# Preparation and table build joined in one block, norm sums moved into the build, filters shifted by one block

## The chip, the core and the metric

The kernel runs on one core of one Trainium2 chip. Its engines are TensorE (PE), VectorE (DVE), ScalarE (ACT), GpSimd (POOL) and the sync engine (SP), which issues most DMAs. The metric is the device time of one execution in microseconds; less is better.

## What is computed

A graph of 6,250 nodes with 128 features each and 200,000 edges sorted by their destination goes through two graph networks, each with a residual and a layer norm behind it. The first is three graph convolutions; the second makes a filter of every edge's weight, multiplies it with the source's features and takes the product over each node's edges.

```python
def graph_conv(x, W, b, act):                    # three times
    h = x @ W
    m = h[src] * norm_src[:, None]               # rsqrt of the out-degree, per edge
    agg = segment_sum(m, dst)
    out = agg * norm_dst[:, None] + b            # rsqrt of the in-degree
    return relu(out) if act else out
def product_net(h, edge_feat, dist):
    bf = exp(coeff * (dist[:, None] - centers[None, :]) ** 2)
    bf = ssp(bf @ W1 + b1)                       # ssp: softplus minus ln 2
    bf = ssp(bf @ W2 + b2)
    cut = where(dist < 5, 0.5 * (cos(pi * dist / 5) + 1), 0)
    agg = segment_prod(h[src] * edge_feat * bf * cut[:, None], dst)
    return ssp(agg @ W3 + b3)
x = layernorm(x + conv(conv(conv(x)))); x = layernorm(x + product_net(x, edge_attr, edge_weight))
```

## The kernel before

The program is a row of blocks. In a block each engine has an instruction list of its own, written out by hand or in loops, and the lists meet only in semaphores; at a block's end all engines meet. All DMAs of SP go through one queue in the order in which they stand; POOL's indirect DMAs (gathers) have another. There is no planner: the order in the text is the order of work on each engine.

**Preparation** (a block of its own, L142 to L260). SP loads the edges as 128 rows of 1,564: destinations (`e_dst`), sources, weights (`e_wt`), and the first destination of every chunk of 128 edges (`fd_i`, single words) and of every row (`e_next`). DVE packs destination and source into one word (`e_pk`, L212, L214), SP stores the packed edges to memory; DVE and ACT work out the cutoff factor of each edge (L216, the sine L248, L240 to L243) and whether an edge has the same destination as the one before it, PE turns the weights (L258), DVE copies them (L224) and SP stores them by step. Each such instruction is 1,564 elements wide.

**Table build** (the next block, L340 to L623). Chunk numbers come first: DVE splits `fd_i` (L403 to L408), makes one-hot rows of it (L411), PE counts them (L555), DVE copies the counts (L416) and sums them up to `chunk_i` (L424). With it POOL gathers 62 chunks of packed edges (L376), nine of them for the first of seven groups. `read_rows(j)` (L451 to L461) splits a group's words, ACT and PE turn them to tables (L514 to L523, L583). Then 28 loop turns of four steps follow: DVE makes the one-hots of a step (`hots`, L432 and L435), PE multiplies them (L599), ACT copies the counts (L540), SP stores them (L352), and PE adds them up for the out-degrees (L564). After the loop, behind each other: the source norms (L476 to L479, root L546), the segment sums of the counts (L483 to L488), the carries between rows (L491 to L493, PE L617 to L622), the pairs (L497, L498) and the step norms (L501, L502, root L548), which SP stores in three DMAs (L356 to L360). Then the block ends and the semaphores are cleared.

**Layers.** 48 blocks n, 16 for each of three layers. In each, PE multiplies the counts of 490 steps, in seven granules of 21 products (L957), with the nodes' features, kept in three bf16 parts `hps`. SP loads one granule ahead (L753). DVE scans the result (L1076), PE multiplies it with the layer's weights. Into the blocks n = 0 to 40 go the edge filters, two per block, at granules 0 and 1 (`slot`): ACT makes the basis of `dist` (L820, L822), PE two products (L932, L940), ACT and DVE the softplus. 82 filters are made there, the other 309 in the next stage. In block 0 the parts of `hps` don't exist yet: for each granule g, DVE scales x (L1092), ACT copies the first part (L868), DVE subtracts (L1100), ACT and DVE make the next two, and PE waits for them before granule g. POOL gathers 49 small tiles of `pairs` (L799) meanwhile; DVE turns them into `last_row` in block 1 (`last_rows`, L1105).

**Edges and end.** A straight stage over 391 blocks of 512 edges gathers node rows (L1306), makes the other filters (L1325 to L1449) and runs the products along (L1434, L1437). A last stage makes the second network's output.

## Time and profile before

| what | us |
|---|---|
| median of 3 runs (lowest, highest) | 5082.86 (5082.14, 5086.49) |
| profiled execution: its time, its span | 5105.77, 5104.0 |
| preparation, until its last DVE instruction ends | 33.5 |
| chunk numbers to the first one-hots of the loop | 33.8 to 76.86 |
| loop of the table build | 76.86 to 862.08 |
| sums behind it, block end | 862.08 to 874.84 |
| first block of the layers | 874.84 to 944.63 |
| other 47 blocks and what follows them | 944.63 to 2638.6 |
| edges | 2638.6 to 4985 |
| last stage | 4985 to 5104 |

In the whole span PE is busy 3802.7 us, DVE 3149.9, ACT 2755.1 and POOL 1897.5. In a table by stage each engine has its busy time and, in brackets, its instructions; PEclk is the granted clock of TensorE, 1.00 being full; then the busy share of the 16 DMA engines and the rate. In a timeline a row is one instruction or a run of like ones (x count): start, length, engine, line, output and inputs, shapes, and in square brackets how long the engine was idle before it and what ended that. SPq and ACTq rows are issues of DMAs, not transfers. A profiled execution takes a little longer than the ones that are timed.

### The profile page before, as it was taken

To read this page: it belongs to the slowest core of one execution; us is meant where nothing else is said; L and a number is where in the kernel's file an instruction comes from. 1 tells how busy PE (TensorE), PEld (TensorE's weight loads), DVE (VectorE), ACT (ScalarE), POOL (GpSimd) and SP (SyncE) were. 2 spreads that over 40 slices of the span, in tenths; PEclk is the share of its full clock that TensorE was granted. 3 is DMA by queue.
4 is the path that set the end of the run, shared out by engine and by line. 5 is a ranking of instruction groups with operands and counts; after the bars stand their busy time and mean duration, and the time that the engine had idled before them with its cause. 6 is when DMAs were issued, how large, how long until landed. Compare 5 with 4: busy or idle time off the path is not lost. (4 is left out here: it accounts for less than half of the span.)

```text
span 5104.0 us, 67054 instructions
## 1 busy us (share of the span) xinstructions
PE 3802.7 (75%) x22995; PEld 2424.4 (48%) x22995; DVE 3149.9 (62%) x5629; ACT 2755.1 (54%) x4313; POOL 1897.5 (37%) x1883
## 2 busy tenths in 40 slices
PE   3888887899999999999965665655656665566642
PEld 2777775444444444444434444443444444444432
DVE  7999997323232323232136777777777777777774
ACT  2666665222222222221017878877878787787863
POOL 4222001300100010001136666666666666666653
PEclk9888988999999999999976777777777677777775
DMA  3333333788877788877755555555555555555541
GB/s 108 132 136 129 126 130 133 227 240 248 243 232 240 244 246 242 255 242 235 224 145 157 171 166 172 167 171 170 168 164 173 172 172 165 166 169 167 172 141 54
DMA packets 641672, 920.47 MB, mean 180 GB/s; under 512 B 70098, under 2 KB 423239, under 8 KB 641431
## 3 DMA queue, kind: packets, MB, share of 16 engines
q1 hardware_dynamic: 550727, 782.65, 48.4%
q0 software_dynamic: 59936, 119.71, 8.8%
q10 hardware_dynamic: 30768, 15.26, 1.0%
q8 instruction: 107, 1.75, 0.1%
q14 instruction: 134, 1.10, 0.1%
HBM read 674.76 MB, written 242.59 MB: 180 GB/s over the span
## 5 line engine op out<-in xcount | busy, mean ns | idle before, releaser
L1306 POOL DMA_INDIRECT hgat<-x_rows,edge_src x1564 | 1497.4, 957 | 826.4 <-issue 453.4
L957 PE MATMUL bank<-gran,hp 128*128 128x490 bf16 x7056 | 1515.1, 373 | 26.6 <-DVE hp L1100 14.2
L957 PEld LDWEIGHTS bank<-gran,hp 128*128 128x128 bf16 x7056 | 678.0, 96 | 817.4 <-issue 29.6
L1373 PE MATMUL bank<-dist,v_sb 128*128 128x512 f32 x618 | 469.6, 849 | 737.9 <-issue 603.7
L1434 DVE TENSOR_SCALAR bank<-rows_e,edge_same,edge_first 128x128 f32<-128x128 f32 x1564 | 644.9, 412 | 121.7 <-DVE rows_e L1437 61.3
L810 POOL DMA_INDIRECT x_sb<-h_rows,last_i x147 | 139.2, 947 | 1540.6 <-DMA h_rows<-h_out 1473.8
L599 PEld LDWEIGHTS bank<-hi_hot,lo_hot 128*128 128x128 bf16 x7840 | 544.9, 155 | 223.3 <-issue 70.8
L599 PE MATMUL bank<-hi_hot,lo_hot 128*128 128x49 bf16 x7840 | 572.9, 219 | 101.4 <-DVE hi_hot L435 99.8
L540 ACT CAST stage<-bank 128x490 bf16<-128x490 f32 x784 | 451.9, 576 | 304.3 <-PE bank L599 304.3
L1386 PEld LDWEIGHTS bank<-v_sb,excess 128*128 128x128 f32 x2472 | 470.7, 262 | 281.8 <-issue 264.1
L1027 DVE TENSOR_SCALAR t<-bank,c_sb 128x512 f32<-128x512 f32 x82 | 61.5, 751 | 855.7 <-PE bank L932 848.3
L1386 PE MATMUL bank<-v_sb,excess 128*128 128x128 f32 x2472 | 477.9, 347 | 118.4 <-issue 117.6
L1437 DVE TENSOR_TENSOR rows_e<-bank,prod_e 128x128 f32<-128x128 f32 x1564 | 455.5, 291 | 163.2 <-DVE bank L1434 66.7
L432 DVE TENSOR_TENSOR lo_hot<-lo_t,rep_lo 128x8960 bf16<-128x8960 bf16 x112 | 539.5, 4817 | 9.9 <-issue 9.8
L1386 PE MATMUL bank<-v_sb,a 128*128 128x128 f32 x2472 | 434.3, 329 | 88.8 <-issue 88.8
L1373 PEld LDWEIGHTS bank<-dist,v_sb 128*128 128x128 f32 x618 | 117.7, 237 | 805.2 <-issue 662.4
L827 ACT ACTIVATE t<-t 128x512 f32<-128x512 f32 x82 | 51.0, 621 | 763.7 <-DVE t L1027 763.7
L1386 PEld LDWEIGHTS bank<-v_sb,a 128*128 128x128 f32 x2472 | 405.4, 246 | 113.7 <-issue 113.6
L1350 ACT ACTIVATE a<-bank,soft_max 128x512 f32<-128x512 f32 x309 | 208.5, 675 | 430.4 <-remote 409.0
L1445 DVE SCALAR_TENSOR_TENSOR bank<-bank,a 128x512 f32<-128x512 f32 x309 | 215.4, 697 | 218.9 <-ACT a L1355 115.1
L564 PE MATMUL bank<-stage,ident_b 128*128 128x490 bf16 x791 | 341.4, 433 | 0.4 <-ACT stage L540 0.4
L1419 DVE TENSOR_TENSOR prod_e<-hgat,efl 128x512 f32<-128x512 f32 x391 | 270.2, 691 | 37.7 <-DVE efl L1449 12.3
(239 smaller groups left out, 4313.9 us busy)
## 6 DMA issues: line engine op xcount, KB each, us to landing
gran<-step_counts SPq DMA_DIRECT2D x336, 857.5 KB
dist<-weight_by_step SPq DMA_DIRECT2D x391, 256.0 KB
running_products<-rows_e SPq DMA_DIRECT2D x391, 256.0 KB
step_counts<-stage SPq DMA_DIRECT2D x112, 857.5 KB
ef<-in_edge_attr SPq DMA_DIRECT2D x391, 224.0 KB
hgat<-x_rows,edge_src POOLq DMA_INDIRECT x1564
kn<-keep_and_norm_of_steps SPq DMA_DIRECT2D x48, 490.0 KB
edge_filter_times_attr<-g_out SPq DMA_DIRECT2D x82, 256.0 KB, 3.6
```

The costliest lines, as they stand in the source:

```text
L432: nc.vector.tensor_tensor(lo_hot[:, r], lo_of.unsqueeze(2).to_broadcast([P, 7, P, GS]), rep_lo[:].unsqueeze(1).to_broadcast([P, 7, P, GS]) ...
L540: nc.scalar.copy(stage[:, u % 2, :, g * GS:(g + 1) * GS], banks[f % 4][:, 0:GS * NT].rearrange("p (s h) -> p h s", h=NT)).then_inc(s_ev, 1)
L564: return nc.tensor.matmul(counts, ident_b[:], stage[:, r, :, g * GS:(g + 1) * GS], start=False, stop=False)
L599: last = nc.tensor.matmul(banks[f % 4][:, s * NT:(s + 1) * NT], lo_hot[:, u % 2, g, :, s], hi_hot[:, u % 2, g * GS + s, 0:NT], start=True, ...
L957: last = nc.tensor.matmul(y, hp[:, 7 * g + i, part, :], gran[:, g, :, i * IS:(i + 1) * IS], start=first, stop=last_)
L1306: pool.indirect_dma_start(out=hgat[:, b % U, c, :], out_offset=None, in_=x1_d, in_offset=bass.IndirectOffsetOnAxis(ap=edge_src[:, b, c:c + ...
L1373: nc.tensor.matmul(ps1[f % R][:], v1_sb[:], dist[:, f % Q], start=True, stop=True).then_inc(s_z14, 1)
L1386: last = nc.tensor.matmul(z[:, c * D:(c + 1) * D], part[:, f % R, c * P:(c + 1) * P], v2_sb[:], start=False, stop=part is a1 and c == C4 - 1)
L1419: nc.vector.tensor_tensor(prod_e[:, b % R], hgat[:, b % U], efl[:, b % U], ALU.mult).then_inc(s_v, 1)
L1434: nc.vector.tensor_scalar(factors[:, c], before, edge_same[:, b, c:c + 1], edge_first[:, b, c:c + 1], ALU.mult, ALU.add).then_inc(s_fac, 1)
L1437: nc.vector.tensor_tensor(rows_e[:, r, c, :], factors[:, c], prod_e[:, b % R, c, :], ALU.mult).then_inc(s_row if c < C4 - 1 else s_run, 1)
L1445: nc.vector.scalar_tensor_tensor(g, g, -LN2, a2[:, f % R], ALU.add, ALU.max).then_inc(s_g4, 1)
```

## The change

The preparation's block is gone. Its instructions stand in the table build's block, so there is one list per engine for both:

- SP loads `fd_i` first, then destinations, sources, `e_next`, weights; stores the packed edges, then loads x, then stores the turned weights.
- DVE does the chunk numbers' one-hots, then the packing, then copies the counts and makes `chunk_i`; then the preparation's other work, then the fills of `stage`, `rep_lo`, `rep_hi` and `strict`, then `read_rows(0)`, and behind it the four instructions of the cutoff factor. Ahead of the loop it waits for the stores of packed edges and weights.
- POOL gathers after `chunk_i` and after the store of the packed edges (a new semaphore, `s_pks`). PE turns the weights after its chunk counts.
- The preparation's tiles lie in space of `lo_hot`, `hi_hot` and `lo_t`.
- The segment sums (`count_sums`) stand in the loop, after group 5; the carries (`carries`) after the third of the four turns of group 6, whose loop is cut in two for it. PE's parts of both stand one piece ahead. After the loop there are the pairs, the step norms and then the source norms.
- In the layers, block 0 has no filters; the filters run in blocks 1 to 41 and their last steps in 42. SP issues the granules of block 0 first, then `kn`, c2, the filter weights and the first two `dist`. ACT makes the first basis ahead of its last copy in block 0. PE has block 1 written out in the first layer and its loop from block 2 on.

```diff
+            lent = lambda tile, start, n, dt: tile[:, start + 2 * EPP * n:start + 2 * EPP * (n + 1)].bitcast(dt)
...
+            e_in, number_k, e_ang = (lent(lo_all, FIRSTS, n, F32) for n in range(3))
+            iota_k = lent(lo_all, FIRSTS, 3, I32)
+            e_dst, e_pk = (lent(hi_all, 0, n, I32) for n in range(2))
...
+            e_wt = lent(lo_t, RB[1] * P, 0, F32)
...
+                    with nc.allow_non_contiguous_dma(reason="first dst of every chunk and of every partition"):
+                        sp.dma_start(fd_i[:, 0:whole], firsts[0:whole * P].rearrange("(t p) o -> p (t o)", p=P)
...
+                    load(e_dst, dst, s_dst)
+                    load(src_k, src, s_src)
...
+                    load(e_wt, edge_weight, s_wt)
+                    sp.wait_ge(s_pk, 1)
+                    sp.dma_start(pk_d.rearrange("(p k) -> p k", k=EPP), e_pk).then_inc(s_pks, 16)
+                    sp.wait_ge(s_iota, 1)
+                    sp.dma_start(run_d[ONES_ROW:ONES_ROW + 1, :], ones_row[:]).then_inc(s_prep, 16)
                     sp.wait_ge(s_xpad, 1)
                     sp.dma_start(x_sb[:, 0:NT - 1, :], x[0:(NT - 1) * P, :].rearrange("(t p) d -> p t d", p=P)
                                  ).then_inc(s_xin, 16)
                     sp.dma_start(x_sb[0:N - (NT - 1) * P, NT - 1, :], x[(NT - 1) * P:N, :]).then_inc(s_xin, 16)
+                    sp.wait_ge(s_wtc, -(-KT // 4))
+                    sp.dma_start(wt_d[0:(KT - 1) * P * P].rearrange("(j k p) -> k j p", k=P, p=P), wt_t[:, 0:KT - 1, :]
+                                 ).then_inc(s_prep, 16)
...
+                    nc.gpsimd.iota(iota_k, [[1, EPP]], base=0, channel_multiplier=0).then_inc(s_iota, 1)
                     pk_rows = pk_d.rearrange("(c e) -> c e", e=P)
                     pool.wait_ge(s_chunk, 1)
+                    pool.wait_ge(s_pks, 16)
...
+                    dve.wait_ge(s_fd, 48)
                     link(nc.vector.memset(fd_i[0:1, 0:1], PADNODE))
...
+                    dve.wait_ge(s_dst, 48)
+                    link(nc.vector.tensor_scalar(e_pk, e_dst, SRCBITS, None, ALU.logical_shift_left))
+                    dve.wait_ge(s_src, 48)
+                    nc.vector.tensor_tensor(e_pk, e_pk, src_k, ALU.bitwise_or).then_inc(s_pk, 1)
+
...
+                    dve.wait_ge(s_wt, 48)
+                    nc.vector.tensor_scalar(e_ang, e_wt, CUTOFF, None, ALU.min).then_inc(s_ang, 1)
+                    nc.vector.tensor_scalar(e_in, e_wt, CUTOFF, None, ALU.is_lt)
+                    nc.vector.tensor_copy(number_k, iota_k)
+                    link(nc.vector.tensor_tensor(e_same[:, 1:EPP], e_dst[:, 1:EPP], e_dst[:, 0:EPP - 1], ALU.is_equal))
...
+                    nc.vector.memset(stage[:, 1], 0.0).then_inc(s_zero, 1)
+                    nc.vector.tensor_copy(rep_lo[:], iota_f[:].unsqueeze(2).to_broadcast([P, P, GS]))
...
                     read_rows(0)
+                    dve.wait_ge(s_sin, 1)
+                    link(nc.vector.tensor_scalar(e_ang, e_ang, 0.5, 0.5, ALU.mult, ALU.add))
+                    link(nc.vector.tensor_tensor(e_ang, e_ang, e_in, ALU.mult))
+                    link(nc.vector.tensor_tensor(same_k, e_same[:], e_ang, ALU.mult))
+                    link(nc.vector.tensor_tensor(first_k, e_ang, same_k, ALU.subtract))
+                    dve.wait_ge(s_pks, 16)
+                    dve.wait_ge(s_prep, 16 * 3)
+                    def count_sums():
+                        dve.wait_ge(s_kt, 1)
+                        nc.vector.tensor_copy(kc[:], banks[4][0:ST, 0:2 * P].rearrange("r (a c) -> r a c", a=2)
+                                              ).then_inc(s_kc, 1)
+                        dve.wait_ge(s_kc, 1)
+                        nc.vector.tensor_tensor_scan(seg_sum[:], kc[:, 0, :], kc[:, 1, :], 0.0, ALU.mult, ALU.add)
+                        nc.vector.tensor_tensor_scan(kept[:], kc[:, 0, :], zeros_r[:], 1.0, ALU.mult, ALU.add)
+                        nc.vector.tensor_tensor_scan(row_sum[:], ones_f[0:ST, :], kc[:, 1, :], 0.0, ALU.mult, ALU.add
+                                                     ).then_inc(s_seg, 1)
+
+                    def carries():
+                        dve.wait_ge(s_tl, 1)
+                        nc.vector.tensor_copy(carry_c[:, 0:1], banks[6][0:ST, 0:1])
+                        link(nc.vector.tensor_copy(tails[:], banks[5][0:1, 0:2 * ST].rearrange("o (a r) -> o a r", a=2)))
+                        nc.vector.tensor_tensor_scan(carry_r[0:1, 1:ST + 1], tails[0:1, 1, :], tails[0:1, 0, :], 0.0,
+                                                     ALU.mult, ALU.add).then_inc(s_car, 1)
+
                     for j in range(7):
                         dve.wait_ge(s_te, fills_to[j])
-                        for a, b in ((4 * j, 4 * j + 1), (4 * j + 1, 4 * j + 4)):
+                        for a, b in parts_of(j):
                             with dve.Fori(a, b) as i:
                                 for u in range(4):
                                     dve.wait_ge(s_fill, i * 28 + 7 * (u + 1))
                                     hots(i, u)
                             if j < 6 and a == 4 * j:
...
+                            if j == 5 and a == 4 * j:
+                                nc.vector.memset(carry_r[0:1, 0:1], 0.0).then_inc(s_cnt, 1)
+                            if j == 5 and b == 4 * j + 4:
+                                count_sums()
+                            if j == 6 and b == 4 * j + 3:
+                                carries()
...
+                    act.wait_ge(s_ang, 1)
+                    nc.scalar.activation(e_ang, e_ang, ACT.Sin, bias=half_pi[:], scale=-math.pi / CUTOFF
+                                         ).then_inc(s_sin, 1)
...
+                    pe.wait_ge(s_const, 1)
+                    pe.wait_ge(s_wt, 48)
+                    for g in range(-(-KT // 4)):
+                        if g >= 3:
+                            pe.wait_ge(s_wtc, g - 2)
...
+                            if j == 5 and a == 4 * j:
+                                turn_counts()
+                            if j == 6 and a == 4 * j:
+                                ends_of_rows()
+                    pe.wait_ge(s_car, 1)
+                    nc.tensor.matmul(banks[6][0:ST, 8:9], carry_r[0:1, 0:ST], ones_f[0:1, 0:1], start=True, stop=True
+                                     ).then_inc(s_cc, 1)
...
-            FREE = FC // FB + 1
+            FREE = FC // FB + 2
...
-                return At(FB * n.const + g, n.reg, FB * n.step)
+                return At(FB * (n.const - 1) + g, n.reg, FB * n.step)
...
-                    load_dist(At(0))
+                    for g in range(NG7):
+                        load_granule(At(0), g)
+                    load_kn(At(0), At(0))
                     sp.dma_start(c2_all[:].rearrange("p (c d) -> p c d", d=D), c2.rearrange(
                         "(a b d) -> a b d", a=1, b=1).to_broadcast([P, C4, D])).then_inc(s_v, 16)
                     for tile, ap in ((c1_sb, col(c1)), (v1_sb, v1), (v2_sb, v2)):
                         sp.dma_start(tile[:], ap).then_inc(s_v, 16)
-                    load_granule(At(0), 0)
+                    load_dist(At(0))
                     load_dist(At(1))
-                    for g in range(1, NG7):
-                        load_granule(At(0), g)
-                    load_kn(At(0), At(0))
                     for tile, ap in zip(ws + bs, (w1, w2, w3, col(b1), col(b2), col(b3))):
                         sp.dma_start(tile[:], ap).then_inc(s_w, 16)
 
                     for n in range(3 * BLOCKS):
                         nxt = At((n + 1) % BLOCKS) if n + 1 < 3 * BLOCKS else None
                         for g in range(NG7):
-                            if g < FB:
+                            if n and g < FB:
                                 slot(filter_of(At(n), g))
                             if nxt is not None:
...
+                            if n == 0 and g == NG7 - 1:
+                                act.wait_ge(s_cst, 1)
+                                basis_of(At(0))
+                            if n and g < FB:
                                 slot(filter_of(At(n), g))
...
-                    pe.wait_ge(s_v, 16 * 4)
 
                     def one_block(k, n, first=False, filters=True):
                         for g in range(NG7):
-                            if g < FB and filters:
+                            if g < FB and filters and not (first and k == 0):
                                 slot(filter_of(n, g))
                             if first:
...
+                            pe.wait_ge(s_v, 16 * 4)
                             pe.wait_ge(s_w, 16 * 6)
-                        pairs_looped = max(0, min(BLOCKS - 2, FREE - 2 - BLOCKS * k) // 2)
+                            one_block(k, At(1))
+                        start = 1 if k else 2
+                        pairs_looped = max(0, min(BLOCKS - 1 - start, FREE - 2 - BLOCKS * k) // 2)
                         if pairs_looped:
                             with pe.Fori(0, pairs_looped) as it:
                                 for h in range(2):
-                                    one_block(k, At(BLOCKS * k + 1 + h, it, 2))
-                        after = min(BLOCKS, max(1 + 2 * pairs_looped, FREE + 1 - BLOCKS * k))
-                        for b in range(1 + 2 * pairs_looped, after):
+                                    one_block(k, At(BLOCKS * k + start + h, it, 2))
+                        after = min(BLOCKS, max(start + 2 * pairs_looped, FREE + 1 - BLOCKS * k))
...
+                    def first_bias():
+                        dve.wait_ge(s_v, 16 * 4)
+                        nc.vector.tensor_scalar(c1_less[:], c1_sb[:], -LN2, None, ALU.add)
+                        nc.vector.tensor_scalar(c1_over[:], c1_sb[:], -SOFT_MAX, None, ALU.add)
+                        link(nc.vector.tensor_scalar(c1_turned[:], c1_sb[:], -1.0, SOFT_MAX, ALU.mult, ALU.add))
...
+                                    first_bias()
```

## Rows read from the trace of the kernel before

**Rows 1.** Busy time by stage, table loop and first layer block; times in us.

```profile
core 0: us, PE busy (x) PEld busy (x) DVE busy (x) ACT busy (x) POOL busy (x), PEclk, DMA share, GB/s
...
76.86:862.08 785.22, 679.55 (x8730) 553.76 (x8730) 777.66 (x354) 478.02 (x824) 130.90 (x40) 0.88 0.32 128
...
874.84:944.63 69.79, 39.50 (x159) 17.27 (x160) 27.09 (x35) 22.41 (x29) 54.81 (x48) 0.72 0.74 210
```

**Rows 2.** Timeline of the preparation up to the loop: start, length, instruction, idle before.

```profile
start us, us, engine line op out<-in xcount [idle before <-releaser]
...
1.75 0.40 SPq L146 DMA_DIRECT2D e_dst<-in_dst  x1
...
4.11 0.40 SPq L160 DMA_DIRECT2D fd_i<-in_dst  x1
...
7.84 0.97 DVE L212 TENSOR_SCALAR e_pk<-e_dst 128x1564 int32<-128x1564 int32 x1 [4.50 <-DMA e_dst<-in_dst]
...
15.23 0.98 DVE L216 TENSOR_SCALAR e_ang<-e_wt 128x1564 f32<-128x1564 f32 x1 [1.83 <-DMA e_wt<-in_edge_weight]
...
31.70 1.79 DVE L243 TENSOR_TENSOR edge_first<-e_ang,edge_same 128x1564 f32<-128x1564 f32 x1
...
35.00 8.59 SPq L346 DMA_DIRECT2D x_sb<-in_x  x1
...
38.55 5.34 DVE L411 TENSOR_TENSOR lo_hot<-fd_f,iota_f 128x1664 bf16<-128x1664 f32 x4
...
45.37 0.21 DVE L416 COPY marks<-bank 128x49 f32<-128x49 f32 x1 [1.49 <-PE bank L555]
...
48.25 1.11 POOL L376 DMA_INDIRECT rows<-packed_edges,chunk_i  x1 [14.21 <-DVE chunk_i L424]
...
60.91 0.81 DVE L451 TENSOR_SCALAR ints<-rows 128x1152 int32<-128x1152 int32 x1 [12.70 <-DMA rows<-packed_edges,chunk_i]
...
65.74 1.36 DVE L461 SCALAR_TENSOR_TENSOR hi_b<-ints,mine 128x1152 bf16<-128x1152 int32 x1
...
66.16 1.75 POOL L376 DMA_INDIRECT rows<-packed_edges,chunk_i  x1 [0.30 <-issue]
...
76.86 4.83 DVE L432 TENSOR_TENSOR lo_hot<-lo_t,rep_lo 128x8960 bf16<-128x8960 bf16 x1 [9.76 <-issue]
```

**Rows 3.** Timeline behind the table loop: VectorE and SP.

```profile
866.11 0.42 DVE L483 COPY kc<-bank 62x256 f32<-62x256 f32 x1 [0.52 <-PE bank L615]
...
869.28 0.15 DVE L496 COPY carry_c<-bank 62x1 f32<-62x1 f32 x1 [0.36 <-PE bank L622]
...
871.61 0.22 SPq L360 DMA_DIRECT2D keep_and_norm_of_steps<-norm_s  x1
```

**Rows 4.** Timeline at the layers' first block; the last row groups line L799.

```profile
878.29 18.88 SPq L753 DMA_DIRECT2D gran<-step_counts  x6
...
886.74 0.15 DVE L1119 TENSOR_SCALAR c_less<-c_sb 128x1 f32<-128x1 f32 x1 [11.63 <-DMA v_sb<-in_L_gnn_W]
...
894.83 7.05 PE L957 MATMUL bank<-gran,hp 128*128 128x490 bf16 x21 [6.00 <-DVE hp L1100]
...
910.36 0.72 ACT L820 ACTIVATE dist<-dist,center 128x512 f32<-128x512 f32 x1 [15.88 <-issue]
...
916.01 28.78 PE L957 MATMUL bank<-gran,hp 128*128 128x490 bf16 x126 [12.38 <-issue]
...
918.96 1.09 DVE L1100 TENSOR_TENSOR hp<-x_sb,hp 128x896 bf16<-128x896 f32 x1 [1.00 <-ACT hp L868]
...
923.06 1.09 DVE L1100 TENSOR_TENSOR hp<-x_sb,hp 128x896 bf16<-128x896 f32 x1 [1.00 <-ACT hp L868]
...
946.38 4.57 PE L957 MATMUL bank<-gran,hp 128*128 128x490 bf16 x21
...
955.97 0.18 DVE L1105 TENSOR_SCALAR has_f<-pairs 128x49 f32<-128x49 f32 x1
...
L799 POOL DMA_INDIRECT pairs<-dges_up_to_and_in_degree,last_i x49: 943/947/1812, 875.5 to 945.3; - x49
```

**Rows 5.** Waits in the edge stage: who, for whom, us in total, times, longest.

```profile
engine line waited for: us in total, times, longest us
...
ACT a L1350 <- remote: 409.0, 79, 19.2
```

More of the change, by code:

```diff
@@ new lines, in _ @@
+                    nc.vector.scalar_tensor_tensor(e_row[:], pcol[:], float(EPP), at_row[:], ALU.mult, ALU.add)
+                    dve.wait_ge(s_next, 48)
+                    link(nc.vector.tensor_tensor(goes_on[:], e_next[:], e_dst[:, EPP - 1:EPP], ALU.is_equal))
+                    link(nc.vector.tensor_tensor(part_same[:], all_same[:], goes_on[:], ALU.mult))
+                    nc.vector.tensor_tensor(part_new[:], goes_on[:], part_same[:], ALU.subtract)
+                    nc.vector.tensor_scalar(part_one[:], goes_on[:], -1.0, 1.0, ALU.mult, ALU.add)
```

289 lines of the change are left out of this document (106 added, 183 removed).

## The prediction

> **What bounds the kernel now.** I read the table of stages first, then the timeline of each stage that the diff touches, then the waits of the rest. The profiled execution took 5105.77 us, a span of 5104.0 and 1.8 around it; the median of the runs shown is 5082.86. I work out the change on the profiled execution and take the sum off the median, 22.9 lower.
>
> The count-table loop is bound by VectorE: busy 777.7 of 785.2 us [rows 1]. Ahead of it stand 76.9 us in which no engine is busy for long: DMA, a chain of short VectorE work and nine gathers follow one another. The first block of the layers lasts 69.8 us with PE busy in 39.5 at a granted clock of 0.72 [rows 1]. The reader is to see three heads or tails in which everyone waits for a chain; the diff touches these three. In the rest PE (layers) and a chain over all engines (edges) set the time, with the same work before and after.
>
> **Part 1, the preparation.** Now it is a program of its own: packing from 7.84, e_ang from 15.23, last instruction 31.70 + 1.79 = 33.5; then chunk numbers, whose one-hots start at 38.55 and take 5.34; the first gather goes out at 48.25, the first rows are read at 60.91, the first large one-hot starts at 76.86 [rows 2]. The change puts the chunk numbers first.
>
> - Landing of fd_i: e_dst, issued first at 1.75, was used at 7.84, 6.1 later. fd_i now stands there, its issues taking 1.8 instead of 1.1. It is 1,563 single words, and its landing isn't visible before. Bounds: 6 (a little below e_dst) and 13.4 (all that packing waited for had landed). I take 8, the nearest row's value.
> - Splitting fd_i takes 0.9 (estimate: six small instructions of 0.15 to 0.2, linked), the one-hots 5.34: 14.3. Packing, 0.97 + 1.79, now stands behind them on VectorE: 17.1. PE's counting falls beside it. From one-hots to gather there are 4.4 us (43.89 to 48.25), of which the first 1.5 was the wait for that counting (45.37), so chunk_i is there at 17.1 + 2.9 = 20.0.
> - The gathers also wait for the store of the packed edges, issued at 17.1. It moves about as much as e_dst, whose load took 6.1 with the start of the queue in it; I take 3.9 (estimate), 6.1 at most: 21.0. So the first gather moves from 48.25 to 21.0.
> - VectorE's moved work between chunk_i and the first rows: from e_ang (15.23) up to the last four full-width instructions (one of 0.97, three of 1.79, so 33.5 - 6.4 = 27.1), 11.9, and the fills of stage and rep_lo, 2.5 (estimate): 14.4. It ends near 34.4, with PE's transposes beside it.
> - Nine gathers took 12.7 from first issue to first use (48.25 to 60.91). Now VectorE works beside them. At 66.16 a gather took 1.75 instead of 0.95 because it stood until the two-input instruction of 65.74 + 1.36 = 67.10 was over, plus 0.81 [rows 2]. The same was seen for gathers in the layers' first block: 49 in 70.8 us, up to 1.81 each [rows 4]. At that pace, one per 2 us while VectorE is busy, seven are out by 34.4 and the last two follow at 1.25: first use at 38.3. Bounds: 33.7 (no obstruction) and 47.1 (none gets through until VectorE is idle at 34.4).
>
> The Trainium skill, SBUF — State Buffer (Who interferes with whom) says that VectorE keeps GpSimd from writing descriptors only in a two-port mode, and that, as it infers, a tensor_tensor with both inputs in SBUF takes the read side alone and doesn't stop them. By it fewer of these instructions would obstruct and first use would be near 36. The row at 66.16 disagrees, as its blocker has two inputs, so I stay with 38.3.
>
> Reading the rows, then the tables through PE and ACT, then the first large one-hot: 60.91 to 76.86, 15.95, with 9.76 of VectorE idle in it [rows 2]. The last four full-width instructions of the preparation go into that idle stretch: 27.1 to 33.5, 6.4 us. They fit; were the idle gone, they would cost 6.4. The start of the loop moves from 76.86 to 54.3, a gain of **22.6** (13.8 to 27.2 by the bounds above).
>
> SP's queue: the load of x moves ahead of the stores of the weights and blocks SP for 8.6 (the 35.00 row). It starts at about 17.5, ends its issues near 27, and the weights' store follows, landing by 35. VectorE now waits for it before the loop, at about 51: 15 us to spare, cost nothing. The sine stands ahead of ACT's tables and is done by 24, long before them.
>
> **Part 2, the sums.** They used to stand behind the loop. From 866.11 to 869.28 VectorE makes the segment sums and carries, from 869.28 to 871.61 the pairs and norms until SP's last store is issued [rows 3]; the layers begin 3.2 later, at 874.84. The loop ends at 862.1 before and after. Moved into the loop, the first piece lengthens it, because VectorE is its bound: 3.2 at most, and 2.4 without the waits for PE (estimate; PE's answers are now long there). After the loop PE makes one small product, VectorE the same 2.3 us chain, then the store: 862.1 + 0.3 + 2.3 + 3.2 = 867.9, against 874.84. The source norms come next to it and end near 866, the last table store has landed by then. Gain 6.9 - 2.4 = **4.5** (bounds 2 and 7).
>
> **Part 3, the layers' first block.** Count from its start, t0 = 874.84.
>
> Now: VectorE waits until 886.74 for filter weights. PE starts at 894.83, runs one granule of 21 products in 7.05, then is idle 12.38 until 916.01, because ACT waited 15.88 for a dist that lay in the queue behind granules (910.36), and runs the other six in 28.78 [rows 4].
>
> Then: VectorE's first scaling starts at t0 + 0.5, and scale, copy, rest, copy, rest (1.09, 0.9, 1.09, 0.9, 1.09, one scaling between) give the first parts at t0 + 5.7. Granules go out each 3.1 (18.88 for six). The first, now issued first, lands by about t0 + 5.5 (3.1 and 2.4 to start, estimate); PE needs one each 4.57 (946.38). Parts come each 4.1 (918.96 to 923.06), also faster than PE. PE starts cold again (7.05 for the first) and takes 27.4 for six: block 0 ends at t0 + 40.2 instead of 69.8. The filter products that it held, one and a half slots of 1.75 (944.63, where block 1 begins, to 946.38), go to block 1: 2.6 [rows 1, 4]. All later filters shift by one block; one more block at the end carries them, one at the start doesn't, so their sum is unchanged. Gross gain 29.6 - 2.6 = 27.0.
>
> What is late next:
>
> - The first dist now stands behind seven granules, kn, c2 and the weights. In the old order c2 and the weights, all issued before the granules, were there only at 886.74, 11.9 after t0 with one dist ahead. I get t0 + 22 for the granules, 31 for dist. ACT wants it in front of its last copy; that makes the last part ready at t0 + 34.1, and PE wants it at t0 + 35.6. 1.5 to spare, up to 4 lost if dist comes 5 later.
> - POOL's 49 pair gathers took 70.8 (875.5 to 946.3) and were needed 11.3 after block 0's end (955.97). VectorE now wants them at t0 + 51.5 and, denser work beside them, gets them at t0 + 76 (15 in the first 31 us, the other 34 at 1.25, 2 to land). Behind last_rows on VectorE stand the filter steps and the scan of block 2. PE wants the first of these at t0 + 77.7. One block of slack swallows the wait but for 0 to 4.
>
> I take 1.7 for both: **25.3** (bounds 18 and 28).
>
> **Sum.** 22.6 + 4.5 + 25.3 = 52.4: 5053.4 in a profiled execution, 5082.9 - 52.4 = **5030.5** as the median.
>
> **Rivals.**
>
> 1. Gathers stand still behind VectorE until 34.4 (first use 47.1). For: the 66.16 row. Against: in the layers' first block they got through one by one between VectorE's instructions. Gain 43.6: 5039.3.
> 2. The head of the layers is held by dist or the pairs. For: both are later than needed by their old order. Against: a block of slack. Up to 7 more: about 5037.
> 3. The loop starts earlier: the 9.76 idle has no instruction of ACT's or PE's filling it fully, and fd_i may land at 6. Up to 6 more: 5025.
> 4. Slower than before: the edge stage. Its code is straight, and its ACT stood 79 times, 409 us, before one line's instruction, 5.2 each, on something the profile can't name [rows 5]. All code ahead of it changes length. From ten such stands more (10.1 x 5.2 = 52.4) the gain is gone; fifteen more give 5030.5 + 78 = 5108.5. Against: the runs of before lie within 4.4 us, so such misses are not loose, and the stage's instructions are untouched.
> 5. It doesn't do what it says: the loop still waits for the weights' store. It decides from the store landing 16 us later than worked out, and each us beyond costs one; at 28 us late: 5043. Against: the engines have 0.8 MB to move then.
>
> By a rule of the Trainium skill, Runtime: NRT & Kernel Launch (Instruction fetch mechanics), crossing a code page is mostly hidden and a taken branch outside the window isn't; the edge stage has no branches, so by it rival 4 would not come. No row here shows which it is.
>
> **How the numbers follow.** Forecast 0.64, rival 1 0.10, rival 2 0.10, rival 3 0.07, rival 4 0.04, rival 5 0.05. A measurement of this kernel tells 0.2%, 10 us, from no change. All but rival 4 and the small chance that the edge stage gives back 42 to 62 us are beyond that: faster 0.94, same 0.03, slower 0.03. Range: all bounds bad give 13.8 + 2 + 18 = 34, 5049; all good 27.2 + 7 + 28 = 62, 5021. The edge stage may shift by a few us either way: 5016 to 5050.
>
> **What would show it.** First gather at 19 to 25; first read of rows at 36 to 40; loop start near 54; loop length 785 + 2.4; 6 us from its end to the layers; first granule product at t0 + 5.7, block 0 over at t0 + 40; layers' block 1 with an idle stretch of VectorE near t0 + 52 to 76 and PE without one. The forecast is wrong if the loop starts after 62, if PE idles over 5 us in blocks 0 to 2, or if the edge stage changes by more than 10 us.

## The result, and the profile after

The changed kernel takes 5050.36 us (median of 6 runs, 5047.3 to 5055.08), the kernel before 5083.19 (6 runs, 5080.0 to 5086.49): ratio 0.9937, 95% interval 0.9926 to 0.9949. It is 32.8 us faster; I had forecast 52.4 and 5030.5, range 5016 to 5050. The direction was right, the size was 19.6 too large, and the range was missed by 0.4.

The profiled execution took 5047.3 us, span 5045.5. Against the 5105.77 of before that is 58.5 less, far more than the medians say. Of it 35.5 lie ahead of the edge stage (first gather of hgat at 2639.25 before, 2603.73 after) and 23.0 in it and behind it, where nothing was changed: the edge stage lasted 2336.8 in the profile of before and 2315.9 in that of after. That is over the 10 us that I had named as a sign of being wrong. The profiled execution of before was 22.9 above the median and that of after 3.1 below it, so I take this for scatter of the edge stage; no second profile on this chip shows it. So the stages ahead of the edges are where the change is to be read.

Busy time by stage, with the columns of [rows 1]: the table loop, the layers' block 0 and the 37 us behind it.

```profile
core 0: us, PE busy (x) PEld busy (x) DVE busy (x) ACT busy (x) POOL busy (x), PEclk, DMA share, GB/s
49.07:836.36 787.29, 683.49 (x8740) 555.71 (x8740) 779.92 (x363) 477.25 (x824) 139.70 (x45) 0.87 0.32 128
844.85:883.34 38.49, 32.41 (x147) 14.57 (x148) 22.28 (x28) 16.32 (x19) 31.14 (x23) 0.88 0.99 297
883.34:920.00 36.66, 17.40 (x65) 6.89 (x63) 3.98 (x5) 3.89 (x6) 25.42 (x27) 0.71 0.48 137
```

The loop starts at 49.07 instead of 76.86 and is 787.3 long instead of 785.2. Block 0 of the layers lasts 38.5 instead of 69.8 [rows 1]. And then block 1, where I had PE busy throughout: 17.4 us of work in 36.7, at a mean granted clock of 0.71.

The preparation (timeline, columns as in [rows 2]): the landing of fd_i, the one-hots, the store of the packed edges, the first gather, the first read of rows, ACT's last table copies, the first large one-hot. The three copies stand in one piece now.

```profile
4.63 0.06 DVE L336 MEMSET fd_i<- 1x1 int32 x1 [0.50 <-DMA fd_i<-in_dst]
...
5.59 5.34 DVE L345 TENSOR_TENSOR lo_hot<-fd_f,iota_f 128x1664 bf16<-128x1664 f32 x4
...
14.42 0.37 SPq L254 DMA_DIRECT2D packed_edges<-hi_hot  x1
...
19.39 1.39 POOL L301 DMA_INDIRECT rows<-packed_edges,chunk_i  x1 [16.46 <-DMA packed_edges<-hi_hot]
...
36.43 0.76 DVE L419 TENSOR_SCALAR ints<-rows 128x1152 int32<-128x1152 int32 x1 [4.72 <-DMA rows<-packed_edges,chunk_i]
...
44.62 2.20 ACT L507 CAST hi_t<-bank 128x1024 bf16<-128x1024 f32 x3
...
49.07 4.83 DVE L400 TENSOR_TENSOR lo_hot<-lo_t,rep_lo 128x8960 bf16<-128x8960 bf16 x1
```

Behind the loop [rows 3]: VectorE's last piece of the sums, the last table store, the last norm store (its issue takes 0.78 us, before 0.22), and the first granule 6.3 later; before, the layers came 3.2 behind that store.

```profile
836.22 0.15 DVE L474 COPY carry_c<-bank 62x1 f32<-62x1 f32 x1 [6.03 <-PE bank L624]
...
836.53 0.33 SPq L271 DMA_DIRECT2D step_counts<-stage  x1
...
838.55 0.78 SPq L279 DMA_DIRECT2D keep_and_norm_of_steps<-norm_s  x1
...
844.85 6.89 SPq L759 DMA_DIRECT2D gran<-step_counts  x5
```

The layers' blocks 0 and 1 [rows 4], timeline of all engines. From 894 on PE runs one or two products and then waits 0.3 to 3 us for nothing that the profile shows ("issue"); ACT's 903.82 had its operands at 889.6, VectorE's 907.28 at 890.4, and both stand idle for 17 and 19 us. PE works without these waits again from 919.87, 4 us behind the start of GpSimd's last gather of pairs (915.74).

```profile
883.34 1.02 PE L938 MATMUL bank<-dist,v_sb 128*128 128x512 f32 x2
...
891.18 3.11 PE L963 MATMUL bank<-gran,hp 128*128 128x490 bf16 x14
...
896.70 0.58 PE L963 MATMUL bank<-gran,hp 128*128 128x490 bf16 x2 [1.73 <-issue]
...
898.10 0.37 PE L963 MATMUL bank<-gran,hp 128*128 128x490 bf16 x1 [0.81 <-issue]
...
903.82 0.67 ACT L852 ACTIVATE xT<-bank,b 128x490 f32<-128x490 f32 x1 [17.19 <-remote]
...
907.28 0.75 DVE L1035 TENSOR_SCALAR t<-bank,c_sb 128x512 f32<-128x512 f32 x1 [19.55 <-issue]
...
915.74 0.94 POOL L804 DMA_INDIRECT pairs<-dges_up_to_and_in_degree,last_i  x1 [0.31 <-issue]
...
919.87 5.54 PE L963 MATMUL bank<-gran,hp 128*128 128x490 bf16 x11 [0.84 <-issue]
```

One scan per block makes a ruler: block 1's follows block 0's by 63.1 us, all others of the layer follow by 35.6. So block 1 loses 27.5. Measured from its own start, the layers' part up to the edges takes 1758.9 instead of 1764.4: 5.5 gained, not 25.3.

### The profile page after: what moved, and what is told of

Read it like the earlier page. It is cut to its first block and busy times, and to the rows that moved or that the text cites. A ratio compares the mean times of both kernels' runs of the same rounds, so it can differ in the third digit from the quotient of the medians.

```text
span 5045.5 us, 66969 instructions
## 1 busy us (share of the span) xinstructions
PE 3789.1 (75%) x22995; PEld 2410.7 (48%) x22995; DVE 3149.6 (62%) x5629; ACT 2753.0 (55%) x4313; POOL 1905.2 (38%) x1883
## 5 line engine op out<-in xcount | busy, mean ns | idle before, releaser
L1396 PE MATMUL bank<-v_sb,a 128*128 128x128 f32 x2472 | 423.5, 323 | 91.1 <-issue 90.9
L1396 PEld LDWEIGHTS bank<-v_sb,a 128*128 128x128 f32 x2472 | 394.7, 240 | 117.5 <-issue 117.2
L1360 ACT ACTIVATE a<-bank,soft_max 128x512 f32<-128x512 f32 x309 | 208.2, 674 | 414.4 <-remote 402.7
```

Of the source, the lines that this page charges most:

```text
L1396: last = nc.tensor.matmul(z[:, c * D:(c + 1) * D], part[:, f % R, c * P:(c + 1) * P], v2_sb[:], start=False, stop=part is a1 and c == C4 - 1)
```

## The experiments

The theories for the lost 20 us. **G**: GpSimd's 49 gathers of pairs, which in block 1 go out one each 1.25 us in an unbroken row (dense, below), hold up the supply of instructions to the other engines. **F**: block 1's code, written out straight for PE, is slow to come in by itself. **W**: VectorE waits for the pairs. **C**, added once the first four had run: it depends on the chip.

The runs fell on four chips. On three of them the kernel before took 4714 to 4724 us (called quick below), on one 5113, near the 5083 of the result, whose chip may be that one or a fifth (both called slow). A time is compared with the kernel before on its own chip only.

**Moving the gathers (e1, e2).** The dense row goes away, each gather of pairs standing behind one of x for layer 2; or it starts after block 1.

```diff
 e1
-for t in range(NT): pool.indirect_dma_start(out=pairs[:, t, :], ...)
 for k in range(1, 4):
     for t in range(NT):
         pool.indirect_dma_start(out=x_sb[:, t, :], ...)
+        if k == 1: pool.indirect_dma_start(out=pairs[:, t, :], ...)
-if n == 1 and g == 3: last_rows()
+if n == BLOCKS + 3 and g == 3: last_rows()
 e2
+pool.wait_ge(s_gran, 7 * 2)
 for t in range(NT): pool.indirect_dma_start(out=pairs[:, t, :], ...)
-if n == 1 and g == 3: last_rows()
+if n == 5 and g == 3: last_rows()
```

> The changed kernel, but the 49 gathers of pairs no longer run densely during the layers' first two blocks: they stand one by one between the gathers of x for the second layer (some three per block), and last_rows moves to block 19. Theory G (the dense gathers of GpSimd hold up the instruction supply of PE, ACT and VectorE in block 1): the one-at-a-time stretch of PE from 894 to 920 is gone, block 1's scan follows block 0's by 36 to 40 us instead of 63.1, and the time falls by 20 to 27 from 5050.4, to 5023 to 5031. Rival F (the straight-line code of block 1 is slow to come in by itself): the stretch stays, 5048 to 5053. Rival W (VectorE waits for the pairs): the stretch of single products stays, only the end of it moves, 5046 to 5050.

> The changed kernel, but the 49 gathers of pairs start only when block 1's products are done, still densely, and last_rows moves to block 5. PE runs a loop there, VectorE and ACT straight code. Theory G: block 1 runs without a stall, and a stall of VectorE and ACT (PE behind them) comes in blocks 2 to 4 instead, 10 to 27 us in all; 5030 to 5050. Rival F: block 1 still stalls by 27, nothing in blocks 2 to 4; 5048 to 5053. A third view, that it takes straight code of PE and gathers together: no stall in either place, 5023 to 5031.

Both ran on a quick chip: e1 4676.7 and e2 4675.1 against 4723.6. All scans of the layer were 35.6 to 36.6 apart in both. That looked like G for e1, but e2 had no stall under its gathers either, and the unaltered kernel hadn't run there.

**The parts by themselves (e3, e4).** Everything ahead of the layers from one kernel, the layers and the rest from the other.

> Parts 1 and 2 of the change alone; the layers and all behind them as before. My theory: the two parts are worth 30 (27.8 at the loop's start, 4.3 behind it, less 2.1 in it), so 5083.2 - 30 = 5053. Rival: the edge stage takes or gives another 10 to 20 with the code's new place, 5035 or 5070.

> Part 3 alone, preparation and sums as before. My theory: block 0 is over at t0 + 39, block 1 stalls by 27, so it brings only 3 to 6: 5077 to 5080. Rival: the stall in block 1 of the changed kernel comes from where parts 1 and 2 put the code or the gathers in time; then there is none here and it brings 25, 5058.

Same chip: parts 1 and 2 alone 4702.1, a gain of 21.5 (ratio 0.9955, 0.9939 to 0.9972); part 3 alone 4699.0, a gain of 24.6 (0.9950, 0.9933 to 0.9966). My 30 for e3 missed: it was worked out with the 27.8 of the slow chip, where the quick one gives 22.9 (table below). My expectation for e4, 3 to 6, missed too, and its rival's 25 came: here part 3 is worth what the prediction had said.

**The unaltered kernels on a quick chip (c1, c2, c3, e7).** e7 has PE's blocks 2 and 3 out of the loop and straight, under the gathers moved as in e2.

```diff
 e7, over e2
-one_block(k, At(1))
-start = 1 if k else 2
+for n in (1, 2, 3): one_block(k, At(n))
+start = 1 if k else 4
```

> The changed kernel, unaltered, beside the others of this call. The last four kernels ran where the kernel before took 4723.6 us, not 5083: the loops had the same durations there to 0.1 us, the edge stage 1991 to 2001 us instead of 2337. Theory C (the stall in block 1 is slow supply of straight-line code, and how slow that is differs from chip to chip, as in the edge stage): where the kernel before takes about 4720, block 1's scan follows block 0's by 36 to 44 us instead of 63.1 and the gain is 40 to 50; where it takes about 5083, it is 63 again and the gain is 33. Rival G (the dense gathers alone make it): 63.1 and a gain of 30 to 35 on either.

> The kernel before, unaltered, for its trace on this chip. Both theories: the same loops as in the first trace to 0.2 us. Theory C: the edge stage is as long as in the other kernels of this call, and the ACT line that stood 409 us before something the profile can't name stands there only where the edge stage takes 2337.

> Again the changed kernel with its gathers of pairs one by one between those of x, beside the unaltered one. Theory G or C: block 1's scan 36.6 behind block 0's on any chip. Against the changed kernel of this call: 20 to 27 us less if that one shows 63 in block 1, 0 to 6 less if it shows 36 to 44.

> The kernel with the dense gathers moved behind block 1, and now blocks 1 to 3 of PE written out straight instead of 2 and 3 in the loop. If it takes straight code of PE and dense gathers at once: stalls of PE in blocks 2 and 3, 2 to 8 us in all where the edge stage takes 2000, 20 to 50 where it takes 2337. If gathers or straight code alone did it, or neither: all scans 35.6 to 37 apart, within 3 us of the kernel with the gathers moved.

The kernel before took 4715.7, the changed one 4668.5 (ratio 0.9895, 0.9879 to 0.9912): 47.2 faster, and 38.6 between its first two scans. So the loss depends on the chip, or on the occasion, as C has it; that it is the supply of code, the other half of C, these runs don't show. e7 on a quick chip tells nothing of the slow one. c3 took 4664.3, e7 4666.4, with all scans 35.6 to 36.6 apart. The changed kernel's block 1 here, PE first, then VectorE (timeline): 105 products in one piece, and VectorE idle from t0 + 48.5 to t0 + 74.8 until the pairs land, which costs PE 1.5. That is the picture that the prediction had drawn.

```profile
895.45 22.23 PE L963 MATMUL bank<-gran,hp 128*128 128x490 bf16 x105
...
920.06 1.16 PE L946 MATMUL bank<-v_sb,s 128*128 128x128 f32 x8 [1.53 <-DVE s L1042]
...
918.57 0.19 DVE L1113 TENSOR_SCALAR has_f<-pairs 128x49 f32<-128x49 f32 x1 [26.34 <-DMA pairs<-dges_up_to_and_in_degree,last_i]
```

The edge stage looks like the same case. The waits of the changed kernel in it (who, for whom, us in total, times, longest), first on the chip of the result, where the stage lasts 2316, then on the quick one, where it lasts 1993:

```profile
PE bank L1383 <- issue: 603.7, 208, 27.3
...
ACT a L1360 <- remote: 402.7, 76, 24.7
...
POOL hgat L1316 <- remote: 331.0, 98, 6.7
```

```profile
ACT a L1360 <- PE bank L1396: 102.3, 67, 7.4
```

These three, ACT's 402.7 us among them [rows 5], are absent on the quick one; PE's weight loads ahead of L1393 have unnamed waits there too, 962.5 us. No run took the gathers out of the edge stage, so that they cause its waits is argued. The same picture stands in the kernel before's own head. In the first trace ACT's table copies, behind which VectorE's 9.76 idle ended [rows 2], come one by one, each after an unnamed wait; on the quick chip (c2) they run in one piece, and the loop starts at 71.76 instead of 76.86. The first trace, then c2:

```profile
71.39 1.01 ACT L523 CAST hi_t<-bank 128x1024 bf16<-128x1024 f32 x1 [2.28 <-remote]
...
74.94 1.01 ACT L523 CAST hi_t<-bank 128x1024 bf16<-128x1024 f32 x1 [2.54 <-remote]
...
76.35 0.37 ACT L523 CAST hi_t<-bank 128x256 bf16<-128x256 f32 x1 [0.39 <-remote]
```

```profile
69.42 2.20 ACT L523 CAST hi_t<-bank 128x1024 bf16<-128x1024 f32 x3
...
71.76 4.83 DVE L432 TENSOR_TENSOR lo_hot<-lo_t,rep_lo 128x8960 bf16<-128x8960 bf16 x1 [4.39 <-ACT hi_t L523]
```

**Again, and part 2 by itself (d1, d2, d3).** d2 is e2's kernel. d3 calls count_sums, carries, turn_counts and ends_of_rows behind the loop:

```diff
 d3
-if j == 5 and b == 4 * j + 4: count_sums()
-if j == 6 and b == 4 * j + 3: carries()
+(behind the loop) count_sums(); carries()
```

> The changed kernel again, on whichever chip. Two chips gave the kernel before 4724 and 4716, and on the second of them this one a gain of 47 and 38.6 between the scans of blocks 0 and 1. Theory C (slow supply of straight-line code, a property of the chip): if the kernel before takes about 4720, again a gain of 45 to 50 and 38 to 39; if it takes about 5083, a gain of 30 to 35 and 60 to 65.

> The changed kernel with the gathers of pairs behind block 1, last_rows in block 5, beside the unaltered one. On a chip where the kernel before takes 4720: VectorE's wait for the pairs in block 1 goes, 1.5 to 3 in the trace of the layers, 1 to 5 faster than the changed kernel. On one where it takes 5083: by G (dense gathers hold the code up) 36.6 in block 1 and 20 to 27 faster; by F (block 1's code is slow to come by itself) 60 to 65 in block 1 and 0 to 4 faster.

> The changed kernel with part 2 half undone: the segment sums and carries run behind the table loop again, with PE's transposes and products for them. My theory of the prediction: the loop is 2.1 to 2.4 shorter, and 4.5 to 6.5 more lie between it and the layers, so the layers start 2 to 4.5 later than in the changed kernel. Rival: the stage behind the loop waits for the last table stores and the barrier whatever VectorE does; then the layers start at the same time or 2 earlier.

The same quick chip, kernel before 4714.1: d1 4666.9, d2 4662.8, d3 4666.8. d3's layers start at 844.30, those of c1 and d1 at 843.76 and 844.66: the rival was right. In d3's tail, timeline of SP's queue, the last norm store goes out at 840.53, 2 to 3 us later than in the changed kernel, and the layers still start at the same time.

```profile
834.93 0.33 SPq L271 DMA_DIRECT2D step_counts<-stage  x1
...
840.53 0.22 SPq L279 DMA_DIRECT2D keep_and_norm_of_steps<-norm_s  x1
...
844.30 1.02 SPq L755 DMA_DIRECT2D gran<-step_counts  x2
```

**The slow chip at last (g1, g2, f2, f3, h1, h2, k1).** g1 (e2's kernel) and g2 (the changed one) met a quick chip and told nothing new: 4662.5 and 4663.6, one execution each. f2 splits each product of blocks 0 and 1, all but a block's first and last, in four; f3 is the same with e2's place of the gathers.

```diff
 f2 in outline, in granule, blocks 0 and 1 only
-last = nc.tensor.matmul(y, hp[...], gran[:, g, :, ...], ...)
+for c0, c1 in ((0, 2), (2, 4), (4, 6), (6, 7)):
+    last = nc.tensor.matmul(y[:, c0 * IS:c1 * IS], hp[...], gran[:, g, c0:c1, ...], ...)
```

> The changed kernel with the dense gathers of pairs behind block 1. Where the kernel before takes about 5083: by G (the gathers hold the code up) the scans of blocks 0 and 1 are 36.6 apart, with or without a stall in blocks 2 to 4; by F (slow supply of straight code by itself) 55 to 65. Where it takes about 4720: 36.6 under both.

> The changed kernel as its control. Where the kernel before takes about 5083: 60 to 65 between the scans of blocks 0 and 1. Where it takes about 4720: 38 to 39.

> The changed kernel, but in blocks 0 and 1 each product of a granule (490 columns) except the first and last of a block is issued as four of 140, 140, 140 and 70, so PE runs some 583 products per block of straight code instead of 147. The sum is the same. If the supply of straight code is near its limit here (theory F for every chip), PE shows stretches of single products with 0.7 to 3 us between them, and block 1 lasts over 100 us. If it is not, PE is bound by the four weight loads per product: 0.10 to 0.13 us each, 60 to 80 us per block, without such gaps.

> The same with the dense gathers behind block 1. By G (gathers hold the code up) it has no gaps where f2 has them, 10 us or more shorter over blocks 0 and 1. By F it has the same gaps. If f2 has none, the two are within 4 us of each other.

> The changed kernel with the gathers of pairs behind block 1 and last_rows in block 5, timed for its size. VectorE's wait of 26 us for the pairs costs PE 2 to 3 in block 1; so 2 to 3 less than the changed kernel, which is 0.05% and likely under what the timing tells apart. Rival: the dense gathers disturb block 2 to 4 and give it back, no difference.

> The changed kernel in the same call, as the other half of that comparison: 46 to 49 under the kernel before where that takes about 4715, 30 to 35 where it takes 5083.

f2, f3, h1 and h2 ran on a slow chip, kernel before 5112.6. The changed kernel (h2) took 5082.1 (ratio 0.9939, 0.9927 to 0.9951), the first result over again; its scans came at t0 + 63.7 and 44.4 behind that, against t0 + 40.8 and 38.6 in c1, so 29 us are lost, with PE's first long wait from 890 on. With the dense gathers moved behind block 1 (h1) it took 5103.8 (0.9980, 0.9971 to 0.9989), 21.7 **slower** than unmoved; none of my numbers for this kernel (e2, d2, g1, h1) said so. Its trace says why. Windows of h1: block 1 is clean, then 49 gathers stand beside 102 products where there is room for 342.

```profile
core 0: us, PE busy (x) PEld busy (x) DVE busy (x) ACT busy (x) POOL busy (x), PEclk, DMA share, GB/s
...
885.00:920.00 35.00, 35.00 (x167) 16.82 (x166) 6.71 (x9) 7.46 (x12) 0.18 (x1) 1.00 0.90 273
920.00:990.00 70.00, 29.37 (x102) 10.69 (x102) 9.81 (x14) 7.77 (x13) 46.45 (x49) 0.63 0.23 62
```

The same kernel, the same windows on a quick chip (e2), with the same 49 gathers:

```profile
885.00:920.00 35.00, 35.00 (x167) 16.80 (x166) 6.71 (x9) 7.46 (x12) 0.00 (x0) 1.00 0.87 266
920.00:990.00 70.00, 70.00 (x342) 34.51 (x341) 19.43 (x28) 17.41 (x28) 46.41 (x49) 1.00 0.82 239
```

In h1 the scans of blocks 1 and 2 are 86.8 apart, all others 35.6 to 36.6. So the stall goes where the dense gathers go; e2's expectation for G had that, and a loss of up to 27, where it was 51. The mean granted clock is lower in the stall (0.63), but even the lower of its two levels, half of full, would leave PE half of the 342 products. Nor can data or another engine hold PE up here: inside a granule of 21 products it waits for no semaphore, and in h1 it has single products there, one each 2.8 us, until the last piece of the block runs through:

```profile
953.82 0.57 PE L964 MATMUL bank<-gran,hp 128*128 128x490 bf16 x1 [2.23 <-issue]
...
986.71 19.63 PE L964 MATMUL bank<-gran,hp 128*128 128x490 bf16 x77 [1.53 <-issue]
```

The queues in 928 to 985, all of it inside the stall (packets, MB, share), h1 and then e2:

```profile
q1 hardware_dynamic: 1229, 1.54, 8.6%
q0 software_dynamic: 1408, 0.05, 3.5%
```

```profile
q0 software_dynamic: 1408, 0.05, 2.3%
q8 instruction: 2, 0.03, 0.3%
q14 instruction: 1, 0.01, 0.0%
```

GpSimd's queue moves the same 0.05 MB in both and the other queues are nearly idle in h1, so it isn't bandwidth. What is missing in h1 as well is a packet of the instruction queue q8, 16 KB each. That looks like code that comes late, but it isn't shown. The next rows are windows from one such packet to the next, first h1 (926.87 to 1006.15), then e2 (927.33 to 955.44):

```profile
926.87:1006.15 79.28, 38.65 (x140) 14.32 (x139) 4.09 (x6) 6.22 (x10) 41.10 (x44) 0.66 0.31 87
```

```profile
927.33:955.44 28.11, 28.11 (x140) 13.58 (x139) 4.00 (x6) 5.78 (x10) 21.10 (x24) 1.00 0.86 244
```

PE does the same 140 products between two packets, stalled or not (in block 1 of the changed kernel 116 with the stall, 875.68 to 926.19, and 127 without it in c1, 875.22 to 901.71). In h1 it ran 77 of them in one piece from 986.71 on, before the next packet came; in the changed kernel it was going again at 919.87 and the next packet came at 926.19. So PE's packets follow its progress, and that none comes is a consequence of the stall rather than its cause. What it is that holds the engines up isn't shown.

Theory F falls with f3, one execution like f2. Four times as many straight-line products without gathers beside them: 593 in 35 us, and six instruction packets of 16 KB in 877 to 924. f2, the same code with the gathers beside it, stalls from 875 on (h2, with a quarter of the code, from 890), so that its scan of block 0 comes at t0 + 87.5 instead of t0 + 42.0. In f3 the stall stands under the moved gathers, as in h1: 86.4 between the scans of blocks 1 and 2. My 60 to 80 us for a block of such products was wrong; block 1 takes 37.6 in both. First f2, then f3; the rows of queues are those of 877 to 924.

```profile
885.00:920.00 35.00, 5.34 (x25) 2.31 (x24) 0.00 (x0) 0.00 (x0) 23.73 (x26) 0.50 0.12 28
...
q1 hardware_dynamic: 3503, 3.61, 24.5%
q0 software_dynamic: 1103, 0.04, 3.1%
```

```profile
885.00:920.00 35.00, 35.00 (x593) 33.40 (x592) 6.72 (x9) 7.46 (x12) 0.00 (x0) 1.00 0.87 260
...
q8 instruction: 6, 0.10, 0.8%
```

**A last try (k1)**, c3's kernel with gathers one by one, meant for a slow chip:

> The changed kernel with its 49 gathers of pairs one by one between those of x of the second layer, some three of each per block. Where the kernel before takes about 5083 to 5113: if only gathers in an unbroken row hold the code up, all scans of the first layer are 35.6 to 36.7 apart, and the time is 25 to 32 below the changed kernel, 55 to 62 below the kernel before (ratio 0.988 to 0.989). If any gather does, the stall comes back in pieces in layer 2, and the ratio is 0.993 to 0.996. Where the kernel before takes about 4715: 48 to 52 below it, as measured before.

It met a quick one: 4668.9 against 4720.4, ratio 0.9893 (0.9877 to 0.9910). On a slow chip it was not run, so that it would win back the 27 us is argued, not shown. One row of f2, on the slow chip, speaks for it: in block 0, where VectorE keeps the gathers at one each 2 us, PE went through 404 of the split products in one piece.

```profile
850.99 24.19 PE L965 MATMUL bank<-gran,hp 128*128 128x490 bf16 x404 [12.41 <-DVE hp L1111]
```

On quick chips the moved versions are 1 to 4 us under the changed kernel, less than these comparisons tell apart, and the version that waits (h1) loses 22 on a slow one. The changed kernel as it stands is the best that was shown on both.

## Why the prediction was wrong

Its steps against the profiled pairs. Slow is the pair of the result, quick is c2 and c1.

| term | predicted | slow | quick |
|---|---|---|---|
| part 1, start of the loop | 22.6 | 27.8 | 22.9 |
| part 2, from there to the layers | 4.5 | 2.2 | 2.4 |
| part 3, layers up to the edges | 25.3 | 5.5 | 25.7 |
| all ahead of the edges | 52.4 | 35.5 | 51.0 |
| medians of the timed runs | 52.4 | 32.8 | 47.2 |

- **Part 1 came out as forecast only on the quick chip, and there in part by luck.** The steps up to the first read of rows were right: first gather at 19.39 (21.0), first read at 36.43 (38.3), 17.0 between them (17.3). fd_i, 1,563 single words, was there at 4.63, sooner than the 6 that I had as its lower bound; the store of the packed edges took back a part (5.0, not 3.9). From the first read to the loop I had kept 15.95, with the four moved instructions in VectorE's idle stretch for nothing. It is 12.6 in the changed kernel on either chip; in the kernel before it is 15.95 on the slow chip and 10.5 on the quick one, where the idle is 4.39 and not 9.76. So on the quick chip the four instructions cost 2.1 of their 6.4, which the earlier read makes good. On the slow chip the gain was 5.2 above the forecast and 0.6 above its bound: 4.8 of the 9.76 stood behind copies of ACT whose wait had no name, and those waits didn't come in the changed kernel. This is what rival 3 had open, and without these 5 us the missing 20 would have been 25.
- **Part 2 was mis-sized.** The loop's growth was right (2.1 against 2.4). The step "then the store" + 3.2 failed: the norm store now goes out 2 us behind the last table store of 857 KB, takes 0.78 to issue, and the layers come 6.3 behind it. Most likely that table store now sets the end, with the small stores in line behind it; no run moved it by itself. d3 shows that half of the moved work could as well stand behind the loop. The net gain of 2.2 is the lower of my two bounds.
- **Part 3: the step that failed** is the sentence that PE goes through block 1 "without" an idle stretch. Block 0 was right: first product at t0 + 6.1 (5.7), its end at t0 + 38.5 (40.2). The wait of VectorE for the pairs was right too and costs 1.5 to 2 where nothing else is in the way (c1). What was missing is that on this chip the other engines get few instructions going while gathers go out densely: 27.5 us lost in block 1, and with the gathers moved (h1) 51 in block 2. In the kernel before, the dense row ran while PE was idle anyway, 12.38 us of it, and broke up when VectorE's parts came, one gather per 2 us [rows 4]; PE then ran without waits. In the changed kernel VectorE is through with its parts by t0 + 31, and then GpSimd goes at 1.25 us each for 43 us beside PE's block 1. The forecast named the condition that would prove it wrong, PE idle over 5 us in blocks 0 to 2, and that is what came.
- **Rival 4** took the 409 us of ACT for misses that hang on where code lies. It gave slower than before, which didn't come. But the waits it pointed at were the sign to read: they are there on the slow chips (402.7 us after, 426.5 in h2) and gone on a quick one. A warning for the failed step stood in my own rows; I used it for the tail of the range and not for the layers, where GpSimd's gathers stand beside the same engines.
- The rule that I cited, the Trainium skill, Runtime: NRT & Kernel Launch (Instruction fetch mechanics), has the crossing of a code page mostly hidden. The packets of 16 KB agree with its page size. No run here speaks against it: f3 takes six packets in 47 us with PE busy throughout, and in h1 the packet before the stall came at 926.87, 7 us ahead of it, and the next one 19 us behind its end. It says nothing of what the runs show, that engines stall beside dense gathers, and my rival 4 was not settled by it.
- The other rivals: gathers that stand still behind VectorE (1) and a late weights' store (5) didn't come; the dist was there 1.5 us late at ACT and held nothing, the pairs cost what I had set aside (2).
- The base: I took the sum off the median although it was worked out on an execution 22.9 longer. The medians bear that out: they differ by 32.8, near the 35.5 ahead of the edges, and not by the 58.5 of the profiled pair.

Shown is that the dense gathers bring the stall on a slow chip: it moved with them from h2 to h1 and from f2 to f3. That it is the issue of instructions that is held up rests on the single products inside a granule and on the unnamed waits of PE, ACT and VectorE at once; f2 stalling earlier than h2 fits it. By what path gathers do it stays open; late packets of PE's code are not it, as far as the traces show. Why on some chips and not on others, and whether it is the chip or something about its state at the time, no run here says.

## What to carry to other kernels

When a change removes idle time, ask what else was using it: here a row of GpSimd's gathers, beside which the other engines hardly advance on some chips, was hidden in a wait that PE had anyway. A wait that the profile can't name, on several engines at once and beside dense gathers, is a price to be carried over to each place where the change lets busy engines and such gathers meet. What is missing during a stall need not be its cause: count what an engine did between two packets before calling them late. And a gain measured on one chip is that chip's: the same edit was worth 30 to 33 us on the slow chips and 47 on a quick one, so time both kernels on each.

## What the runs showed of the hardware

- Chips, or occasions, differ by 8% on this kernel (4714 to 4724 and 5083 to 5113). A block of the layers without a stall lasts 35.6 on all; the edge stage, straight code under 1,564 gathers, lasts 1987 to 2001 or 2316 to 2346.
- Beside gathers at 1.25 us each on a slow chip PE gets one or two products per 1.4 to 2.8 us, in stretches that begin 3 to 22 us after the dense row does (f2: 872.55 and 875.35; h1: 920 and 934; after: 872.50 and 894) and end 4 to 7 us after the last gather starts (after: 915.74 and 919.87; h1: 980.12 and 986.71). Beside gathers at one each 2 us PE had no such waits (f2, block 0).
- Between two instruction packets of 16 KB PE did the same 140 products, in 79 us with a stall (h1) and in 28 without (e2).
- A load of 1,563 single words, issued at 1.75 to 3.24, was in use at 4.63.
